# Self-attention step loop: scores issued a step ahead, softmax sum moved ahead of the output addition

## The reference

```python
qkv = x @ W_w.T + W_b                       # x is layer-normalised, 16 heads of 16
attn = einsum('bhqd,bhkd->bhqk', q, k) / sqrt(d)
attn = where(causal, -inf, attn) + bias     # position bias
w = softmax(attn, axis=-1)
o = einsum('bhqk,bhkd->bhqd', w, v)
y = x + (o @ proj_w.T + proj_b)
return layernorm(y) * ln_g + ln_b           # then added to the residual
```

## Time and profile before

| | |
|---|---|
| median of 3 runs | 1731.11 us (lowest 1729.69) |
| profiled execution | 1730.49 us |
| its span in the profile | 1728.7 us |
| TensorE busy | 1450.7 us (84%) |
| VectorE busy | 1081.6 us (63%) |
| ScalarE busy | 900.0 us (52%) |
| GpSimd busy | 839.4 us (49%) |

### The profile page before, as it was taken

The page is one execution under the profiler, slowest core; times in us unless marked ns, Lnnn a source line. Parts: engine busy times, 40 slices in busy tenths (PEclk is TensorE's granted clock), DMA queues, the critical chain, the costliest instruction groups (busy, mean ns, idle before and its releaser), DMA issues. The chain is left out here.

```text
span 1728.7 us, 55875 instructions
## 1 busy us (share of the span) xinstructions
PE 1450.7 (84%) x24601; PEld 1018.8 (59%) x24601; DVE 1081.6 (63%) x1736; ACT 900.0 (52%) x1196; POOL 839.4 (49%) x555
## 2 busy tenths in 40 slices
PE   3789999999999999999999999999655655457607
PEld 2357777677776777766777767777424444333206
DVE  7656666666666666666666666666353444586985
ACT  1446555566556665566665556656433322143752
POOL 5567655666655666556665566653053443202000
PEclk9899999999999999999999999999876876678958
DMA  5544544334444344443454534543122110010001
GB/s 171 134 118 103 126 115 136 105 98 123 120 112 133 98 117 123 114 134 98 108 129 108 143 99 101 128 115 69 31 70 52 26 38 1 1 37 0 1 0 49
DMA packets 90688, 154.94 MB, mean 90 GB/s; under 512 B 17280, under 2 KB 55816, under 8 KB 90448
## 3 DMA queue, kind: packets, MB, share of 16 engines
q1 hardware_dynamic: 89088, 150.40, 33.4%
q10 hardware_dynamic: 1360, 0.98, 0.2%
HBM read 60.95 MB, written 2.20 MB: 37 GB/s over the span
## 5 line engine op out<-in xcount | busy, mean ns | idle before, releaser
L639 DVE TENSOR_REDUCE MXP<-W_PS 128x1 f32<-128x512 f32 x768 | 499.2, 688 | 283.4 <-PE W_PS L451 283.4
L535 ACT ACTIVATE PR<-S_PS 128x1024 f32<-128x1024 f32 (+1 forms) x416 | 424.9, 1023 | 258.6 <-PE S_PS L399 250.8
L345 POOL TENSOR_TENSOR K_HI<-K,MCOL 128x512 f16<-128x512 f32 (+1 forms) x224 | 219.0, 978 | 425.3 <-ACT K L543 424.0
L347 POOL TENSOR_TENSOR K_LO<-K,K_HI 128x512 f16<-128x512 f32 (+1 forms) x224 | 291.8, 1302 | 17.6
L451 PE MATMUL W_PS<-STK,QS 105*128 105x512 f16 (+1 forms) x1024 | 269.8, 335 | 9.0 <-POOL STK L372 4.8
L399 PE MATMUL S_PS<-QS,STK 105*128 105x128 f16 (+1 forms) x3328 | 256.0, 220 | 1.0 <-DVE QS L653 1.0
L414 PEld LDWEIGHTS O_PS<-PR,V 128*17 128x17 f32 x13312 | 191.0, 98 | 79.2 <-issue 59.1
L414 PE MATMUL O_PS<-PR,V 128*17 128x64 f32 x13312 | 231.3, 220 | 7.6 <-ACT PR L535 7.5
L434 PE MATMUL W_PS<-WV_HI,CTX_HI 128*128 128x256 f16 (+1 forms) x832 | 228.3, 274 | 1.6 <-DVE WV_LO L612 1.4
L434 PE MATMUL W_PS<-WV_HI,CTX_LO 128*128 128x256 f16 (+1 forms) x832 | 227.7, 274 | 0.0
L434 PE MATMUL W_PS<-WV_LO,CTX_HI 128*128 128x256 f16 (+1 forms) x832 | 227.6, 274 | 0.0
(11 more groups left out here) (243 smaller groups left out, 1713.3 us busy)
## 6 DMA issues: line engine op xcount, KB each, us to landing
CTX<-in_ctx_t SPq DMA_DIRECT2D x64, 800.5 KB, 5.9
STK<-K_HI SPq DMA_DIRECT2D x256, 128.0 KB, 2.6
STK<-K_HI SPq DMA_DIRECT2D x256, 72.1 KB, 2.1
STK<-K_LO SPq DMA_DIRECT2D x128, 128.0 KB, 2.6
STK<-K_LO SPq DMA_DIRECT2D x128, 72.1 KB, 2.1
QSTK<-STK SPq DMA_DIRECT2D x12, 192.0 KB
SQS<-QK_HI SPq DMA_DIRECT2D x32, 64.0 KB, 2.0
KZ<-QK_HI SPq DMA_DIRECT2D x64, 32.0 KB, 2.0
```

Of the source, the lines that this page charges most:

```text
L345: pool.tensor_tensor(K_HI[:, m, lo:hi], k32, zero, ALU.add).then_inc(k_hi, 1)
L347: pool.tensor_tensor(K_LO[:, m, lo:hi], k32, K_HI[:, m, lo:hi], ALU.subtract).then_inc(k_lo, 1)
L535: nc.scalar.activation(PR[0:m, par, :], S_PS[par][0:m, :], ACT.Exp).then_inc(p_sb, 1)
L639: dve.tensor_reduce(MXP[:, j, at:at + 1], bank[:, :], AX.X, ALU.max).then_inc(mx_done, 1)
```

## The change

Four moves inside the step loop; no instruction is added, removed or resized.

1. TensorE: the scores of tile 0 are issued ahead of the loop, and step s issues those of s+1. Their waits move with them: for the bias addition of s (`t_a`), since `S_PS` has one buffer, and for `stacked[r]`, one step earlier.
2. VectorE: sum and reciprocal of s-1 come directly behind the maxima of s, ahead of the output addition of s-3, the units of `BESIDE` and the rows of `ADDED`.
3. ScalarE: the units `TN` and `QK` of `BESIDE[s]` come ahead of the exponential of s.
4. The units `XT` stay behind it.

```diff
--- before.py
+++ after.py
@@ -997,21 +997,26 @@
                         last = pe.transpose(bank[:, (2 * k + s) * P:(2 * k + s + 1) * P], XN[:, t, k * P:(k + 1) * P], CST[:, C_ID:C_ID + P])
                 last.then_inc(sm["xt_ps"], 1)
 
+        def scores(t):
+
+            r, lo = t // 4, t % 4 * P
+            if t % 4 == 0:
+                pe.wait_ge(stacked[r], 16 * PARTS)
+            need(pe, sm["t_a"], t)
+            for j in range(PAIRS):
+                for w in range(2):
+                    cols = slice(lo + w * SQ, lo + (w + 1) * SQ)
+                    for a in range(2):
+                        last = pe.matmul(S_PS[SQ * a:SQ * (a + 1), (2 * j + w) * SQ:(2 * j + w + 1) * SQ], SQS[0:96, r % 2, j, cols],
+                                         KZ[0:96, r % 2, j, a, cols], start=True, stop=True, skip_group_check=True)
+            last.then_inc(sm["s_ps"], 1)
+
         for x in SETUP:
             setup(x)
+        scores(0)
         for s in range(STEPS):
-            if live(s):
-                r, lo = s // 4, s % 4 * P
-                if s % 4 == 0:
-                    pe.wait_ge(stacked[r], 16 * PARTS)
-                need(pe, sm["t_a"], s)
-                for j in range(PAIRS):
-                    for w in range(2):
-                        cols = slice(lo + w * SQ, lo + (w + 1) * SQ)
-                        for a in range(2):
-                            last = pe.matmul(S_PS[SQ * a:SQ * (a + 1), (2 * j + w) * SQ:(2 * j + w + 1) * SQ], SQS[0:96, r % 2, j, cols],
-                                             KZ[0:96, r % 2, j, a, cols], start=True, stop=True, skip_group_check=True)
-                last.then_inc(sm["s_ps"], 1)
+            if live(s + 1):
+                scores(s + 1)
             if live(s - 2):
                 t = s - 2
                 if t == 0:
@@ -1120,6 +1125,9 @@
                 for w in range(2):
                     rows = slice(64 * w, 64 * w + 64)
                     nc.scalar.activation(VS[rows, t % 2, w, :], V[rows, t, :], ACT.Copy).then_inc(sm["vs"], 1)
+            for x in BESIDE.get(s, []):
+                if x[0] != "XT":
+                    setup(x)
             if live(s):
                 act.wait_ge(sm["t_sub"], s + 1)
                 nc.scalar.activation(T[:, s % 3], T[:, s % 3], ACT.Exp, scale=1 / 16).then_inc(sm["t_exp"], 1)
@@ -1129,7 +1137,8 @@
             if s == 17:
                 normal_again(range(4, 10))
             for x in BESIDE.get(s, []):
-                setup(x)
+                if x[0] == "XT":
+                    setup(x)
         act.wait_ge(sm["chain"], CHAIN * 4)
         normal_again(range(10, 14))
         setup(ENDING[0])
@@ -1293,6 +1302,13 @@
                 dve.wait_ge(sm["t_a"], s + 1)
                 need(dve, sm["t_sub"], s - 1)
                 dve.tensor_reduce(MX[:, s % 2], T[:, s % 3], AX.X, ALU.max).then_inc(sm["t_max"], 1)
+            if live(s - 1):
+                t = s - 1
+                dve.wait_ge(sm["t_exp"], t + 1)
+                need(dve, sm["t_norm"], t - 1)
+                dve.tensor_reduce(SM[:, t % 2], T[:, t % 3], AX.X, ALU.add).then_inc(sm["t_sum"], 1)
+                dve.wait_ge(sm["t_sum"], 2 * t + 1)
+                dve.reciprocal(SM[:, t % 2], SM[:, t % 2]).then_inc(sm["t_sum"], 1)
             if live(s - 3):
                 t = s - 3
                 dve.wait_ge(sm["y_ps"], t + 1)
@@ -1305,13 +1321,6 @@
                 dve.wait_ge(sm["y_stat"], 11)
                 scale_rows(*NORMS[0], 0)
             add_rows(ADDED.get(s, ()))
-            if live(s - 1):
-                t = s - 1
-                dve.wait_ge(sm["t_exp"], t + 1)
-                need(dve, sm["t_norm"], t - 1)
-                dve.tensor_reduce(SM[:, t % 2], T[:, t % 3], AX.X, ALU.add).then_inc(sm["t_sum"], 1)
-                dve.wait_ge(sm["t_sum"], 2 * t + 1)
-                dve.reciprocal(SM[:, t % 2], SM[:, t % 2]).then_inc(sm["t_sum"], 1)
             if s == 16:
                 dve.wait_ge(sm["y_stat"], 14 + 10)
                 scale_rows(*NORMS[0], 1)
```

## The result

The changed kernel takes 1662.38 us (median of 4, 1661.87 to 1662.77) against 1731.11 before, the median of three executions; a fourth took 2875.70 us and is left out. The ratio is 0.9602, 95% interval 0.9583 to 0.9621. The profiled execution took 1662.44 us.

A forecast was written before the change was run, and what follows sets the result against it. No engine is full; a chain of waits with two false links sets the pace. Savings of 24 (steps 0 to 7), 24 (8 to 12) and 17 (13 to 16) make 65 off 1730.49: 1666 us, range 1654 to 1694.

The forecast's parts named there:

- The low end of the range: Whole kernel: every loop step with TensorE at 2.4 GHz saves 76 us, giving 1654.
- The circles: Plain steps: four closed chains of waits, the longest setting the pace, 6.2 to 7.4 us a step.
- circle (a): Plain steps: two-step chain from output addition through multiplication and projection to the next but one; 12.4 us, 6.2 each.
- the high level: TensorE at 2.4 GHz: transposes 1.02 us, scores 0.69, products 1.01, projection 1.83; mostly expected in plain steps.
- both links: Old loop: sum behind output addition, scores behind transposes; neither needs the other, in steps of 11.3 us on average.
- the walk through the lists: Steps 0 to 7: instruction lists followed from 1300.24; step 8 starts at about 1371 instead of 1394.74, 24 us saved.
- the low level: TensorE at 1.2 GHz: transposes 1.97 us, scores 1.06, products 1.85, projection up to 2.74.
- The page against it: Steps 13 to 15: GpSimd's work beside the rows may block VectorE, 0 to 5.7 us; taken as 0.
- The low clock: Rival, loop steps: TensorE's clock stays low, saving only 42 us, 1689; chance 0.16.
- The stacks: Rival, scores of tiles 4, 8, 12: three stack transfers lie open, 13 us slower, 1744; chance 0.03.
- the alternation rival: Rival, loop: TensorE and VectorE still alternate, 9.0 us a step in steps 8 to 12, 1699; chance 0.09.
- the eviction rival: Rival, steps 0 to 7: moved evictions delay exponential and sum, stretch stays at 94.5 us, 1690; chance 0.10.

The follow-up runs named there:

- Addition early: The changed kernel with GpSimd's addition to X in steps 0 to 3 in place of 8 to 11: 1665.20 us, ratio 0.9622.
- sum only: The kernel before with only the VectorE move, sum and reciprocal ahead of the output addition: 1677.29 us, ratio 0.9687.
- Scores only: The kernel before with only the TensorE move, scores issued a step ahead: 1733.86 us, ratio 1.0011.
- Filled gaps: The changed kernel plus unused matmuls, 30 behind the transposes of step 13 and 24 ahead of those of step 15: 1660.80 us, ratio 0.9593.
- rows first: The changed kernel with the statistics chain and the rows of ADDED ahead of the output addition in steps 13 to 16: 1658.78 us, ratio 0.9580.

## Why the prediction was right, by its steps

**Time.** 1666 forecast, 1662.4 measured; saved 65 forecast, 68.0 measured between the two profiled executions. That is closer than its parts: steps 0 to 7 gave 2.6 us more than forecast, steps 8 to 12 1.6 more, the end 1.0 more and steps 13 to 16 2.4 less. The low end of the range was added up wrongly. Five steps at 6.2 save 25.5 us, and with 24 + 5 and 17 + 2 that makes 73.5, not 76, so the low end should have been 1657.6 and not 1654.

**Steps 8 to 12.** The circles held. 6.5 a step was a hedge; circle (a) at the high level said 6.2 and the steps average 6.18 (30.88 for five). "Addition early" showed that (a) sets them, "sum only" that its circle with the scores inside is 8.13.

**What bounds the kernel before** was read wrongly in one point. The prediction called both links false and hung the scores into the circle. "Scores only" shows that the circle of before runs through the output addition alone: 1.97 + 1.08 + 1.85 + 2.03 + 0.81 + 1.56 + 1.95 = 11.2 from the prediction's own prices, beside 11.3 measured. Part 2 is worth 54 us alone and part 1 nothing alone; on top of part 2 the scores become the circle (8.13), and taking them out brings the remaining 17 us (1677.3 to 1659.8 without part 3).

**Steps 0 to 7.** 24 forecast, 26.6 measured, and the walk through the lists met the starts within a microsecond at tiles 1 to 3: 1306, 1314, 1324 against 1305.6, 1313.7, 1323.5. Steps 3 and 4 were counted as 8.3 and 8.2 and took 6.95 and 7.22; that is most of the 2.6. It missed the size of part 3's cost: about 1 us of delay in steps 4 to 6 was counted, but not the clock that the delay brings down. Part 3 gains 6 us alone and costs 2.6 on top of the other two, by the medians and by steps 0 to 7 of the profiles (67.9 against 65.3); the intervals of the two ratios overlap.

**Steps 13 to 16.** 17 forecast, 14.6 measured. The mis-sized term is the projection at the low level, taken as 2.4 in both places:

```profile
1414.03 1.07 PE L1010 MATMUL S_PS<-KZ,SQS 96*64 96x64 f16 x32 [7.69 <-DVE T L1300]
...
1416.87 3.07 PE L1042 MATMUL Y_PS<-WP,OT 128*128 128x256 f32 x8
...
1431.23 1.97 PE L1055 MATMUL T_PS<-CST,T 128*128 128x128 f32 x8 [6.30 <-POOL T L1189]
...
1436.16 3.66 PE L1042 MATMUL Y_PS<-WP,OT 128*128 128x256 f32 x8
```

After idle stretches of 7.69 and 6.30 us it takes 3.07 and 3.66, together 1.9 us more than counted. "Filled gaps" confirmed the cause: without the idle stretches both took 1.99.

**The page against it.** I took 0 of a possible 5.7 us and wrote that no row of before showed the pair. In step 15 after the change (GpSimd, then VectorE):

```profile
1429.28 1.90 POOL L1189 TENSOR_TENSOR T<-T,SM 128x1024 f32<-128x1024 f32 x1
...
1429.41 2.05 DVE L1282 SCALAR_TENSOR_TENSOR XN<-XN,MV,LG 128x256 f32<-128x256 f32 x1
...
1431.49 0.48 DVE L1285 SCALAR_TENSOR_TENSOR X<-XN,RS,X 128x256 f32<-128x256 f32 x1
```

The row addition of 0.47 takes 2.05 and ends as the multiplication ends: 1.58 lost, once. By the Trainium skill (SBUF — State Buffer, Who interferes with whom) a VectorE instruction with two SBUF inputs contends with a GpSimd instruction that reads SBUF; the trace agrees, and "rows first" shows it again three times. In step 15 VectorE was ahead of the products and the projection, so the loss was hidden.

The trace of before did have a row of the kind, though not in a row addition: the first chain of step 16 (GpSimd, then VectorE):

```profile
1509.29 1.90 POOL L1180 TENSOR_TENSOR T<-T,SM 128x1024 f32<-128x1024 f32 x1 [11.31 <-DVE SM L1314]
...
1509.87 1.35 DVE L1255 TENSOR_SCALAR VE<-MV 128x10 f32<-128x10 f32 x1
```

It ends with the multiplication as well. After the change nothing runs on GpSimd there and the same instruction takes 0.17. These 1.18 us account for the 1.0 saved behind the chain, which the forecast carried over unchanged.

**Rivals.** The low clock did not come: 1.00 in steps 8 to 12. The stacks were never waited for after the first. Nothing had to be taken from the alternation rival: bias additions wait for no scores. Of the eviction rival a small part is real: the setup steps pay for part 3, but 2.6 us, not 24.

## What to carry to other kernels

In a software pipeline on strict instruction lists, write down the circles with their lengths in steps and add them up from row starts; the longest wait in a list names the engine that is early, not the link to cut, and a second cut can be worth nothing until the first is made. Where TensorE's clock is part of the circle, price a delay twice, once as itself and once as the matmuls behind it at the low level. Where such a gap cannot be closed, filling it with matmuls that compute nothing can pay: 4 us of 43 here.

## What the runs showed of the hardware

A delay of one microsecond, from 0.77 to 1.72 us of idle TensorE, came before a fall to the low level in steps 5 and 6, where eight projection matmuls then took 3.46 and 3.68 in place of 1.99. Idle time alone does not tell the level: the same 1.46 and 0.49 us stood ahead of products of 1.09 us in one profile and of 1.85 in another. A three-operand VectorE instruction of 0.47 to 0.48 us was held to 2.00 to 2.05 by a GpSimd multiplication of 1.90, and GpSimd's own took 2.08 when VectorE had started first.
